# A macaron layer on one core: the first step's rows pass in two halves, and attention's row products stand one unit later

## The reference

```python
x = x + 0.5 * ffn(layernorm(x)); x = x + attention(layernorm(x)); x = x + 0.5 * ffn(layernorm(x))

# ffn: 16 routed experts (2 of 4 groups, then the best 4), 2 shared ones, width 128
h = jnp.einsum('td,edf->etf', x, gate_w); u = jnp.einsum('td,edf->etf', x, up_w)
y = jnp.einsum('etf,efd->etd', jax.nn.silu(h) * u, down_w)
routed = jnp.einsum('etd,te->td', y, combine)
sh = jax.nn.silu(x @ sh_gate_w) * (x @ sh_up_w) @ sh_down_w

# attention: 32 heads of 4, no softmax
a = jnp.einsum('bthd,bshd->bhts', q, k); ctx = jnp.einsum('bhts,bshd->bthd', a, v)
# group norm of ctx over each head and all positions, then ctx @ out_w.T + out_b
```

## Time and profile before

| what | before |
|---|---|
| median of 3 runs | 649.80 us (649.76 to 650.26) |
| the profiled execution: its time, its span | 649.93 us, 648.2 us |
| TensorE busy | 636.3 us, 98% |
| VectorE, POOL, ScalarE busy | 522.5 us, 463.9 us, 394.4 us |
| DMA engines, mean rate | 145 GB/s |

### The profile page before, as it was taken

How to read it: one execution, slowest core, us unless ns; L and a number is a source line. 1 busy time by engine, 2 the same in 40 slices (tenths; PEclk the granted TensorE clock), 3 DMA queues, 4 the chain that set the end, 5 groups by cost and what they waited for, 6 DMA issues and landing times.

```text
span 648.2 us, 9973 instructions
## 1 busy us (share of the span) xinstructions
PE 636.3 (98%) x2927; PEld 526.5 (81%) x2927; DVE 522.5 (81%) x1546; ACT 394.4 (61%) x783; POOL 463.9 (72%) x401
## 2 busy tenths in 40 slices
PE   8999999999999999999999999999999999999997
PEld 7888888888878888788887888878888888888886
DVE  6898888787968879678797798877988878777674
ACT  4876656566575656755667556575565656655554
POOL 6997767767766677676767667676777776777664
PEclk9999999999999999999999999999999999999999
DMA  8727362634438244383353742726627263451710
GB/s 235 261 78 261 67 260 55 213 94 125 178 87 257 73 118 178 82 214 130 93 202 81 187 145 52 272 71 147 208 52 276 50 207 121 117 203 26 277 33 32
DMA packets 128342, 94.26 MB, mean 145 GB/s; under 512 B 84112, under 2 KB 110624, under 8 KB 128288
## 3 DMA queue, kind: packets, MB, share of 16 engines
q1 hardware_dynamic: 128288, 93.63, 47.1%
HBM read 81.55 MB, written 12.06 MB: 144 GB/s over the span
## 4 chain that ended last, share of the span: by engine, by line
PE 83%; DVE 7%; ACT 4%; POOL 3%; issue 2%; DVEq 0%; ACTq 0%; POOLq 0%
PE gateP L547 9%; PE gateP L551 9%; PE upP L551 9%; PE gateP L548 9%; PE upP L547 9%; PE upP L548 9%; PE yP L551 9%; PE yP L547 8%; PE yP L548 8%; ACT XA L863 2%; DVE A L1385 1%; PE attP L617 1%; POOL A_lo L426 1%; ACT XN L830 1%; PE yP L674 1%
## 5 line engine op out<-in xcount | busy, mean ns | idle before, releaser
L426 POOL TENSOR_TENSOR A_lo<-A,A_hi 128x512 fp32r<-128x512 f32 x287 | 369.7, 1296 | 131.9 <-ACT A_hi L907 131.6
L933 ACT ACTIVATE gateP<-gateP 128x512 f32<-128x512 f32 x252 | 146.5, 581 | 196.8 <-PE gateP L551 196.2
L1324 DVE TENSOR_TENSOR T<-gateP,CB 128x512 f32<-128x512 f32 x252 | 173.6, 689 | 96.0 <-ACT gateP L933 92.3
L907 ACT CAST A_hi<-A 128x512 fp32r<-128x512 f32 x287 | 175.9, 613 | 12.5 <-DVE A L1385 11.6
L1385 DVE TENSOR_TENSOR A<-upP,T 128x512 f32<-128x512 f32 x254 | 173.8, 684 | 2.9
L547 PE MATMUL gateP<-XT_hi,W_hi 128*128 128x512 f32 x288 | 116.3, 404 | 0.0
L547 PE MATMUL yP<-A_hi,W_hi 128*128 128x512 f32 x288 | 112.4, 390 | 0.0
L551 PE MATMUL gateP<-XT_lo,W_hi 128*128 128x512 f32 x288 | 112.3, 390 | 0.0
L551 PE MATMUL yP<-A_lo,W_hi 128*128 128x512 f32 x288 | 112.3, 390 | 0.0
L548 PE MATMUL gateP<-XT_hi,W_lo 128*128 128x512 f32 x288 | 112.2, 389 | 0.0
L548 PE MATMUL yP<-A_hi,W_lo 128*128 128x512 f32 x288 | 112.1, 389 | 0.0
(11 more groups left out here) (233 smaller groups left out, 628.4 us busy)
## 6 DMA issues: line engine op xcount, KB each, us to landing
CB<-combT SPq DMA_DIRECT2D x126, 512.0 KB, 7.2
y_rows<-YB SPq DMA_DIRECT2D x60, 64.0 KB, 1.9
YP<-y_rows SPq DMA_DIRECT2D x15, 256.0 KB, 2.8
x_rows<-XN SPq DMA_DIRECT2D x13, 256.0 KB, 2.3
XB<-x_rows SPq DMA_DIRECT2D x52, 64.0 KB, 2.3
xa_rows<-XA SPq DMA_DIRECT2D x4, 512.0 KB, 5.0
W_in<-xa_rows SPq DMA_DIRECT2D x16, 128.0 KB, 2.9
out_dram<-X SPq DMA_DIRECT2D x7, 256.0 KB, 9.1
```

Source lines behind the costliest of these rows:

```text
L426: pool.tensor_tensor(A_lo[:, slot, :], A[:, slot, :], A_hi[:, slot, :].bitcast(F32), ALU.subtract).then_inc(low_done, 1)
L907: act.copy(A_hi[:, v % SLOTS, :], A[:, v % SLOTS, :]).then_inc(high_done, 1)
L933: act.activation(dst, gateP[u % 2][:, :], ACT.Silu).then_inc(silu_done, 1)
L1324: dve.tensor_tensor(T[:, u % TS, :], silu, weights, ALU.mult).then_inc(gate_weighted, 1)
```

## The change

Five things are changed.
- **First step.** The four tiles XN are transposed in two halves, the first into prepP and the second into another bank, upP[1]. VectorE copies, ScalarE casts and VectorE subtracts by halves, with semaphores of their own; the logits of the first two tiles wait for the first half only. One filler product instead of two stands before the transposes, none behind them.
- **Weights.** The three loads of the shared experts' weights are started by ScalarE, behind its first silu, and no longer by SP ahead of the routed experts' weights. POOL subtracts the weights of units 2 to 5 before the next step's rstd and shift, not after. The gate product of unit 5 stands before the spreads of comb.
- **Attention rows.** TensorE's products of XA move from u = 10 to u = 11, ScalarE's copy GS from 11 to 12, s_row and Gn from 12 to 13, VectorE's two operations on GS from 12 to 13.
- **Normalisation.** In the first step of an attention pair, `normalise` runs at w = 10 and not 9.
- **Mf** goes to a part of the PSUM bank attP and not to SBUF.

```diff
-    WARM, FILL = 13, 2
+    WARM, FILL = 13, 1
@@ SyncE
-            for i, w in enumerate((sh_gate_w, sh_up_w)):
-                sp.dma_start(W_in[:, 0:SHARED, i, :],
-                             w.rearrange("d (s f) -> d s f", s=SHARED)).then_inc(w_in[0], 16)
-            sp.dma_start(W_in[:, 0:SHARED, 2, :],
-                         sh_down_w.rearrange("(s f) d -> f s d", s=SHARED)).then_inc(w_in[0], 16)
@@ GpSimd
+            for unit in range(SHARED, SHARED + SPREAD):
+                split_low(unit)
+
             pool.wait_ge(xn_ready, 2)
             step_rstd(1)
-            for unit in range(SHARED, 10):
+            for unit in range(SHARED + SPREAD, 10):
                 split_low(unit)
@@ TensorE
+            def transpose_first():
+                for h, bank in enumerate((prepP, upP[1])):
+                    pe.wait_ge(xn_ready, h + 1)
+                    for j in range(TILES // 2):
+                        mm = pe.transpose(bank[:, j * P:(j + 1) * P], XN[:, h * TILES // 2 + j, :], ident[:, :])
+                    if h == 0:
+                        mm.then_inc(first_turned, 1)
+                    else:
+                        mm.then_inc(xt_done, 1)
...
                 if t < 2:
-                    pe.wait_ge(xt_ready, t + 1)
-                    if t == 1:
+                    if t == 0:
+                        pe.wait_ge(first_copied, 1)
+                    else:
+                        pe.wait_ge(xt_ready, t + 1)
                         pe.wait_ge(route_seq, 2)
                     for j in range(TILES):
+                        if t == 0 and j == TILES // 2:
+                            pe.wait_ge(xt_ready, 1)
...
-                if u == 10:
+                if u == 11:
                     pe.wait_ge(xa_ready, b + 1)
...
                 gate(4)
+                gate(5)
                 pe.wait_ge(route_seq, ROUTE_OPS)
                 spread(0)
                 spread(1)
                 transpose_weights(0)
-                gate(5)
...
             keep_busy(FILL)
-            transpose_next(0)
-            keep_busy(FILL)
+            transpose_first()
             pe.wait_ge(setup_sb, 1)
@@ ScalarE
-                if u == 11:
+                if u == 12:
                     act.wait_ge(att_pe, ATT_PE * b + 1)
                     act.copy(GS[:, :], attP[:, 0:P + 1]).then_inc(att_act, 1)
-                if u == 12:
+                if u == 13:
...
-                    if w in ((15, 16) if early else (9,)) and not last:
+                    if w in ((15, 16) if early else (10 if attention and s == 0 else 9,)) and not last:
...
+            for i, w in enumerate((sh_gate_w, sh_up_w)):
+                act.dma_start(W_in[:, 0:SHARED, i, :],
+                              w.rearrange("d (s f) -> d s f", s=SHARED)).then_inc(w_in[0], 16)
+            act.dma_start(W_in[:, 0:SHARED, 2, :],
+                          sh_down_w.rearrange("(s f) d -> f s d", s=SHARED)).then_inc(w_in[0], 16)
...
-            next_high(0, 0)
+            for h, cols in enumerate(HALVES):
+                if h == 0:
+                    act.wait_ge(first_copied, 1)
+                    act.copy(XT_hi[:, 0, cols], XT[:, cols]).then_inc(first_high, 1)
+                else:
+                    act.wait_ge(xt_ready, 1)
+                    act.copy(XT_hi[:, 0, cols], XT[:, cols]).then_inc(xt_hi_ready, 1)
@@ VectorE
-                if u == 12:
+                if u == 13:
                     dve.wait_ge(att_act, ATT_ACT * b + 1)
...
-                    dve.scalar_tensor_tensor(Mf[:, :], rv[:, :], bk[:, :], attP[:, 0:P],
+                    dve.scalar_tensor_tensor(attP[:, P:2 * P], rv[:, :], bk[:, :], attP[:, 0:P],
                                              ALU.mult, ALU.add).then_inc(att_seq, 1)
                     dve.wait_ge(att_seq, v + 11)
-                    dve.tensor_tensor(Mm[:, :], Mf[:, :], blk1[:, :], ALU.mult).then_inc(att_seq, 1)
+                    dve.tensor_tensor(Mm[:, :], attP[:, P:2 * P], blk1[:, :], ALU.mult).then_inc(att_seq, 1)
...
+            lo, hi = HALVES
+            dve.wait_ge(first_turned, 1)
+            dve.tensor_copy(XT[:, lo], prepP[:, lo]).then_inc(first_copied, 1)
             dve.wait_ge(setup_sb, 1)
             dve.wait_ge(stats_seq, 5)
             dve.tensor_reduce(sums, both, AX.X, ALU.add).then_inc(stats_seq, 1)
+            dve.wait_ge(xt_done, 1)
+            dve.tensor_copy(XT[:, hi], upP[1][:, lo]).then_inc(xt_ready, 1)
...
-            dve.wait_ge(xt_done, 1)
-            dve.tensor_copy(XT[:, :], prepP[:, :]).then_inc(xt_ready, 1)
+            dve.wait_ge(first_high, 1)
+            dve.tensor_tensor(XT_lo[:, 0, lo], prepP[:, lo], XT_hi[:, 0, lo].bitcast(F32), ALU.subtract)
...
+            dve.wait_ge(xt_hi_ready, 1)
+            dve.tensor_tensor(XT_lo[:, 0, hi], upP[1][:, lo], XT_hi[:, 0, hi].bitcast(F32),
+                              ALU.subtract).then_inc(xt_lo_ready, 1)
...
-            dve.wait_ge(xt_hi_ready, 1)
-            dve.tensor_tensor(XT_lo[:, 0, :], prepP[:, :], XT_hi[:, 0, :].bitcast(F32),
-                              ALU.subtract).then_inc(xt_lo_ready, 1)
```

More of the change, by code:

```diff
@@ L247, in macaron_kernel @@
         attended = sem("attended")
+        first_turned, first_copied, first_high = sem("first_turned"), sem("first_copied"), sem("first_high")
         spread_square = sem("spread_square")
```

## The result

The changed kernel takes 646.25 us (median of five runs, 645.92 to 647.59) beside 649.87 for the kernel before (649.76 to 650.26) on the same chip: ratio 0.9947, 95% interval 0.9933 to 0.9962. It is faster, by 3.6 us, but 3.5 us above the predicted 642.8 and outside the range of 641.9 to 644.6. The profiled execution took 646.15, span 644.4 (before: 649.93, span 648.2).

A forecast was written before the change was run, and what follows sets the result against it. TensorE was taken as the bound, losing time only in waits: 649.93 less 5.94 (XA gaps), 1.04 (Mm gaps) and 0.05 (first step) gives 642.90, or 642.8 as a median; range 641.9 to 644.6 us.

The forecast's parts named there:

- The failed step: First step, second X tile's transfer: loads moved to ScalarE's queue were taken to cost it 0.
- The bound: First step: if up to 256 KB cut in beside the second X tile, XN is 0.9 us late.
- step +0.3 to +0.6: First step: cost in us of XN being 0.9 us late, after the slack behind it.
- rival C: First step: interleaving queues or a later W_hi make XN and the first split late, 643.1 to 643.9; chance 0.13.
- signs of being wrong: Waits for A_lo beyond 1 us, weighted gates or CB; Mm over 1 us; XN starting after 6.9.
- the signs for the weighted gates, CB and Mm: Attention steps: weighted-gate waits in the second unit after L617, a CB wait at the next step's start, Mm over 1 us.
- The XA gap: Attention, before L617: TensorE's four waits for ScalarE's XA rows go, 5.94 us in all.
- the lags that I looked for: Attention: ScalarE's silu 1.6 us late, GS copies a unit later, SP's row store 0.67 later; all expected to fit.
- The Mm gap: Attention, before L632: with Mf in PSUM, Mm takes 0.28 us instead of 1.25 and four waits go, 1.04 in all.
- the shape's own cost would have stayed: Attention, Mm: were 1.25 us the cost of two SBUF tiles, it would stay, the sum -5.94 and not -6.98.
- 0.5 us of head start comes down to 0.05: First step: TensorE's earlier start is mostly eaten by POOL's later rstd and shift, leaving a 0.05 us gain.
- the case for which the prediction gives +0.54: First step: POOL's third split starts at 11.82 as before, so the step costs 0.54 us more.

The follow-up runs named there:

- e9: Changed kernel with eight filler products before the first transposes and POOL waiting for XN ahead of its first weight split: 644.27 us, ratio 0.9918.
- e1: Changed kernel with the three shared-weight loads back on SP's queue, ahead of the routed weights: 642.26 us, ratio 0.9883.
- e3: Kernel before with only the three shared-weight loads moved to ScalarE's queue: 654.17 us, ratio 1.0063.
- e2: Changed kernel with eight filler products instead of one before the first transposes: 644.89 us, ratio 0.9923.
- e6: Kernel before with only Mf moved to PSUM: 648.33 us, ratio 0.9976.
- e11: Changed kernel, ScalarE's queue kept, with the second X tile's load issued directly behind the first: 642.24 us, ratio 0.9884.
- e10: Changed kernel with the shared loads on SP's queue and POOL's rstd and shift back behind the second split: 641.56 us, ratio 0.9875.
- e4: Changed kernel with SP waiting for the second X tile before it starts the routed loads: 643.98 us, ratio 0.9910.
- e12: Changed kernel with ScalarE's three shared loads held until the second X tile has landed: 650.27 us.

## Why the prediction was wrong

**The failed step** is this one: "What they may cost is the second X tile's transfer ... If up to 256 KB more cut in, XN is 0.9 us late ... If nothing cuts in, 0. I take 0: the shared gate weights were already in flight beside it." It failed three times over.
- *The choice.* The reason given for 0 was that a load was already beside the tile. But before, the only loads near the tile came from the same queue, behind it. ScalarE's issues stood at 1.07, 1.77 and 2.42 in the trace of after, beside its table load and not behind its first silu at 2.3: two of the three were ahead of the tile's issue at 2.17. And 256-KB routed loads took the place of 128-KB shared ones behind it.

```profile
0.80 1.28 ACT L992 ACT_TABLE_LOAD   x1 [0.80 <-PEq L1538]
1.07 0.66 ACTq L995 DMA_DIRECT2D W_in<-in_L_ffn_sh_gate_w_dram  x1
1.77 0.62 ACTq L995 DMA_DIRECT2D W_in<-in_L_ffn_sh_up_w_dram  x1
2.09 0.20 ACT L992 ACTIVATE warm<-half 128x1 f32<-128x1 f32 x1
2.42 0.62 ACTq L997 DMA_DIRECT2D W_in<-in_L_ffn_sh_down_w_dram  x1
```

- *The bound.* 256 KB at 274 GB/s gave 0.9 us. ScalarE's loads are 384 KB, and four routed loads of 256 KB each are issued from 2.64 to 6.30, before the tile lands at 7.69; the delay was 1.98. The bound was reckoned for one neighbour, at the throughput of the kernel before. The Trainium skill (DMA: Bandwidth & Descriptors, "Issuing engines are not separate DMA queues") says that such transfers share the same 16 engines and interleave; the runs agree in that each set of loads delays the tile, by 0.63, 0.74 and, both together, 1.40 to 1.98 us. I had cited it and set it at 0.13.
- *What a late tile does.* I passed it on as "step +0.3 to +0.6", a delay less its slack. The runs show a mechanism that enlarges it: TensorE out of filler idles (1.67 us), the granted clock is 0.50 for six us behind it, casts and splits wait for slow gate products, and 1.98 become 3.87. e9 shows the step without it: 0.93 behind a tile 1.40 late. So rival C had the late tile right but not the idle time and the clock behind it, and a price of 0.3 to 1.1 over the forecast, where it was 4.0 (e1 against the changed kernel, e3 against before: 4.3).

Of its signs of being wrong the prediction met one, XN starting after 6.9 (8.48); TensorE's longest wait for A_lo was 0.2 us, and the signs for the weighted gates, CB and Mm did not come.

**The XA gap**: right. No wait is left, XA is complete ahead of XN, either edit does it alone (6.1 and 6.7 us). None of the lags that I looked for, silu, GS, the stores on SP, gave a wait. **The Mm gap**: right, 0.29 for 0.28. That it was a wait for POOL, and not the shape's cost, is as the Trainium skill says (SBUF — State Buffer, "Who interferes with whom"); the 910 and 413 ns of the kernel before and the XN of 1.10 and 2.48 us (e9, e2) agree, and e6 fits it. The prediction's sentence that the shape's own cost would have stayed was wrong, and no time hung on it. My account of that rule was too short, though: an instruction with one SBUF input was to be free of the lock, and XN has one tensor input. The same section goes on to name `tensor_scalar` among the operations that can hold the shared pair with a single input, in its 2-port modes; 1.10 against 2.48 us agrees with that, though no run shows the mode itself. **The size** of both was short by 0.7 to 1.0 of 6.98: I counted idle time, not the slower products behind each gap.

**The first step's own edits**: the step "0.5 us of head start comes down to 0.05" has the right place and was slightly off. I let the third split start 0.54 earlier, at 11.28. In e1 it started at 11.82 as before, the case for which the prediction gives +0.54, a second down product at 23.57; it was at 23.45. In e11 it started at 11.24 and the second down product at 22.84, for 23.03. So the split's start, and with it the step, moves by half a microsecond with when the weights land. That POOL's order costs something is shown by e10, which undoes it: 0.44 in the traces, 0.7 by the medians, for the 0.5 that the prediction let it eat.

With the failed step taken out, the prediction's 642.8 stands beside a measured 642.26. So the error of 3.5 us is +4.0 for the queue, about +0.4 for the first step as e1's trace has it (23.45 for 23.03), and -0.7 to -1.0 for the attention gaps. The last two have opposite signs, so that 642.26 comes so near to 642.8 is partly luck.

**Open**: whether the two shares of the tile's delay (0.63 and 0.74) add, and why the delay with both ranges from 1.40 to 1.98; no run has varied bytes and order apart. Also why e9's median lies 1.1 above what its trace accounts for: its slowest execution had a lower clock, but 644.04 came with 1.00.

## What to carry to other kernels

When loads go to another engine's queue, ask first what transfer on the path is issued after them or close ahead of them, and issue that one first: here one line moved up made the second queue free of cost, and without it one edit ate half of what three others gave. Price a delay of the first tile not by the delay but by what TensorE does meanwhile: if it idles, multiply by what its clock does afterwards. An operation moved on a helper engine is free only where that engine was waiting anyway; POOL's 1.3 us were nearly free at 10.1 us and cost 0.4 (traces) to 0.7 (medians) at 15.7. And a half microsecond read from one trace of a program's start is no more than what two executions of the same code differ by.

## What the runs showed of the hardware

- Granted clock: behind an idle time of 1.67 us in the first step it was 0.50 (1.2 GHz) from 10 to 16 us, back at 1.00 from 17 on. It fell in the traces of e2 (TensorE idle for 1.4 us), e3 (3.0), e4 (0.6 and 1.4) and e12 (5.8) too, and not in those of e1, e9, e10 and e11, whose waits there were 0.1 to 0.4 us. In e12 a first wait of 0.6 us was followed by 1.00 for four us. The XA gaps of 1.3 us before, amid dense work, were followed by 1.00.
- VectorE's four XN operations (SBUF to SBUF, one tensor operand each) took 1.10 us alone and 2.47 or 2.48 beside POOL's two-operand split; Mm 1.25 beside it with both operands in SBUF, 0.29 with one in PSUM. A 128x256 subtraction with both operands in SBUF took 0.91 beside POOL's and 0.41 alone.
- The same 26 warm-up products of TensorE ended between 6.46 (e10) and 7.34 us (e11) in the traces.
- The issues of 256-KB loads on SP, 0.51 us each at first (3.19 and 3.73), took 2.02 and 2.57 at 4.28 and 6.34 in the changed kernel; before, the same queue went from 0.51 to 0.89 and 1.15 at 6.83 and 7.77.
